# A projection moved ahead between two attention half-steps, and three PSUM banks taken in turn, in a fused attention and feed-forward block

## What is computed

```python
q = proj(query, Wq, bq)
k = proj(key, Wk, bk)
v = proj(value, Wv, bv)
scores = jnp.einsum('bhqd,bhkd->bhqk', q, k) / jnp.sqrt(jnp.asarray(dk, q.dtype))
p = jax.nn.softmax(scores, axis=-1)
x = jnp.einsum('bhqk,bhkd->bhqd', p, v)
x = x.transpose(0, 2, 1, 3).reshape(B, S, D)
return jnp.einsum('bsd,ed->bse', x, Wo) + bo
...
x = x + jnp.tanh(g_xattn[0]) * _L0_xattn_ref(_layernorm(x, axis=-1), ctx_1024, ctx_1024, ...)
x = x + jnp.tanh(g_ffn[0]) * _L0_ffn_ref(_layernorm(x, axis=-1), ...)
```

## Time and profile before

| | us |
|---|---|
| median of 3 runs | 1734.7 (1734.4 to 1735.49) |
| the profiled execution, its time | 1731.45 |
| its span, first to last instruction | 1729.3 |
| PE busy | 1601.9 (93%) |
| DVE busy | 1302.7 (75%) |
| ACT busy | 840.5 (49%) |
| POOL busy | 558.9 (32%) |

### The profile page before, as it was taken

How to read it: one execution, slowest core, us unless ns; L and a number is a source line. 1 busy time by engine, 2 the same in 40 slices (tenths; PEclk the granted TensorE clock), 3 DMA queues, 4 the chain that set the end, 5 groups by cost and what they waited for, 6 DMA issues and landing times.

```text
span 1729.3 us, 31276 instructions
## 1 busy us (share of the span) xinstructions
PE 1601.9 (93%) x11748; PEld 752.0 (43%) x11748; DVE 1302.7 (75%) x2085; ACT 840.5 (49%) x1122; POOL 558.9 (32%) x782
## 2 busy tenths in 40 slices
PE   4879999999999999999999999985999999989888
PEld 2334544444445444444454444433444444434333
DVE  5638788787887887878878778676687778778766
ACT  4443534535336344353353533524677777757440
POOL 5423514335234242351432523212000000008778
PEclk9989999999999999999999999999899999999999
DMA  8668769788687687886968777635344552027996
GB/s 243 167 173 180 176 160 206 166 199 171 179 182 185 171 191 179 193 176 170 204 160 203 174 180 141 168 71 198 116 183 182 207 200 98 25 82 296 424 413 229
DMA packets 301108, 320.75 MB, mean 185 GB/s; under 512 B 176432, under 2 KB 225584, under 8 KB 298032
## 3 DMA queue, kind: packets, MB, share of 16 engines
q1 hardware_dynamic: 299248, 318.72, 67.8%
q10 hardware_dynamic: 1728, 0.27, 0.1%
HBM read 180.49 MB, written 100.27 MB: 162 GB/s over the span
## 4 chain that ended last, share of the span: by engine, by line
PE 44%; issue 25%; DVE 11%; DMA 7%; ACT 6%; POOL 4%; SPq 3%; POOLq 0%; ACTq 0%; DVEq 0%
PE bank L1492 10%; PE bank L1380 10%; PE bank L1382 9%; PE bank L1381 9%; PE spair L1469 5%; DMA x<-out_dram 4%; DVE mx L1032 4%; POOL yh L712 3%; ACT pr L755 2%; PE spair L1444 2%; DMA stacks<-mT 2%; SPq L412 1%; ACT wf L825 1%; DVE wi L1120 1%; DVE bst L982 1%
## 5 line engine op out<-in xcount | busy, mean ns | idle before, releaser
L1032 DVE TENSOR_REDUCE mx<-spair 128x4 f32<-128x1024 f32 x256 | 301.1, 1217 | 33.9 <-PE spair L1444 33.4
L755 ACT ACTIVATE pr<-spair 128x1024 f32<-128x1024 f32 x256 | 258.0, 1019 | 125.4 <-PE spair L1469 125.4
L1009 DVE SCALAR_TENSOR_TENSOR parts<-bank,bqk,parts 128x512 f16<-128x512 f32 x128 | 96.0, 750 | 177.8 <-ACT parts L744 176.4
L1600 PE MATMUL spair<-xqT,wgT 128*128 128x512 bf16 x704 | 182.5, 382 | 1.0 <-ACT xqT L910 1.0
L1600 PE MATMUL spair<-xqT,wuT 128*128 128x512 bf16 x704 | 182.1, 381 | 0.0
L1469 PE MATMUL spair<-stacks 128*128 128x256 f16 x1024 | 154.2, 277 | 24.8 <-DMA stacks<-mT 14.4
L744 ACT ACTIVATE parts<-bank,bqk 128x512 f16<-128x512 f32 x128 | 87.7, 685 | 153.4 <-PE bank L1382 153.4
L868 ACT ACTIVATE sil<-spair,gsc 128x512 f32<-128x512 f32 x176 | 118.3, 680 | 78.8 <-PE spair L1600 78.7
L618 POOL TENSOR_TENSOR cl<-cbuf,ch 128x512 f16<-128x512 f32 x64 | 79.0, 1235 | 236.4 <-ACT ch L732 236.4
L712 POOL TENSOR_TENSOR yh<-yh,x 128x512 f32<-128x512 f32 x64 | 134.7, 2136 | 48.7 <-DVE yh L1328 25.0
L1492 PE MATMUL bank<-pr,v 128*32 128x256 f32 x2048 | 137.9, 387 | 12.3 <-ACT pr L755 7.6
(11 more groups left out here) (187 smaller groups left out, 3324.4 us busy)
## 6 DMA issues: line engine op xcount, KB each, us to landing
stacks<-qk_spill SPq DMA_DIRECT2D x384, 128.0 KB, 4.0
qk_spill<-parts SPq DMA_DIRECT2D x64, 512.0 KB, 5.1
x<-out_dram SPq DMA_DIRECT2D x32, 1024.0 KB, 11.1
h_spill<-hb SPq DMA_DIRECT2D x10, 2816.0 KB, 9.2
xbuf<-in_x_dram SPq DMA_DIRECT2D x16, 1024.0 KB, 7.2
cbuf<-in_ctx_dram SPq DMA_DIRECT2D x16, 1024.0 KB, 6.7
xres<-in_x_dram SPq DMA_DIRECT2D x16, 1024.0 KB, 5.6
out_dram<-xres SPq DMA_DIRECT2D x16, 1024.0 KB, 4.6
```

Of the source, the lines that this page charges most:

```text
L755: act.activation(pr[:, u % 4, :, :, :].rearrange("p a b q -> p (a b q)"), spair[u % 2][:, :, :].rearrange("p a q -> p (a q)"), ACT.Exp, sc ...
L1009: dve.scalar_tensor_tensor(out=parts[:, c, 2 * w + 1, :], in0=pj[(g + 1) % 3][:, :], scalar=bqk[:, w, c:c + 1], in1=parts[:, c, 2 * w, :], ...
L1032: dve.tensor_reduce(mx[:, h:h + 2, b, :], spair[u % 2][:, :, :].rearrange("p a (q k) -> p a q k", q=KH), AX_X, ALU.max).then_inc(max_done, 1)
L1600: last = pe.matmul(spair[k % 2][:, s, :], w[:, t, kc * P:kc * P + P], xqT[:, par, kc, :], start=(kc == 0), stop=(kc == KC - 1))
```

## The change

Four things change, all in attention bodies with a new group i.

1. On PE `qk(i, 2)` stands between `score(j, 1)` and `score(j, 2)`. In the loop over g each step takes the projection that the next step had: `qk(i, g + 3)` for g = 0 to 4, `vproj(i, 0)` for g = 5 and `vproj(i, 1)` for g = 6, where no projection stood within the loop.
2. After the loop there is one projection less. `max_pair(i, 0)` follows directly; `vproj` 2 and 3 have pairs 1 and 2 behind them, the four `oproj` pairs 3 to 6, and pair 7 follows pair 6.
3. The three banks are taken strictly in turn by the 16 projections of a body, through `turn_bank`. Since 16 is not a multiple of 3, the first bank moves by one from body to body.
4. The waits of `vproj` 0 to 2 name the `qk_low` that empties their bank in the new turn.

```diff
+        def turn_bank(i, k):
+            if i == 0:
+                return pj[(k + 1) % 3 if k < 8 else k % 3]
+            return pj[(i + k) % 3]
+
         def x1_bank(j, t):
-            return pj[t % 2] if j == LAST else pj[t % 3]
+            return pj[t % 2] if j == LAST else turn_bank(j + 1, 12 + t)
...
             def vproj(i, t, par):
                 if t < 3:
-                    wait(pe, qk_lo, i * 8 + (8, 6, 7)[t])
+                    wait(pe, qk_lo, i * 8 + ((8, 6, 7) if i == 0 else (6, 7, 8))[t])
                 else:
                     wait(pe, v_ready, i * NT + 1)
-                three(pj[(2 + t) % 3][:, :],
+                three(turn_bank(i, 8 + t)[:, :],
...
                 score(j, 0)
                 score(j, 1)
+                if i is not None:
+                    qk(i, 2, par, before)
                 for g in range(NGR - 1):
                     score(j, 2 * g + 2)
                     pv(j, g)
                     score(j, 2 * g + 3)
-                    if i is not None and g + 2 < 8:
-                        qk(i, g + 2, par, before)
+                    if i is not None:
+                        if g + 3 < 8:
+                            qk(i, g + 3, par, before)
+                        else:
+                            vproj(i, g - 5, par)
                     if i is None and g >= NGR - 3:
                         oproj(j, g - (NGR - 3), None)
                 if i is not None:
-                    vproj(i, 0, par)
                     max_pair(i, 0)
                 pv(j, NGR - 1)
                 if i is not None:
-                    for t in range(1, NT):
+                    for t in range(2, NT):
                         vproj(i, t, par)
-                        max_pair(i, t)
+                        max_pair(i, t - 1)
                 for t in range(NT) if i is not None else range(2, NT):
                     oproj(j, t, i)
                     if i is not None:
-                        max_pair(i, NT + t)
+                        max_pair(i, NT - 1 + t)
+                if i is not None:
+                    max_pair(i, 7)
```

More of the change, by code:

```diff
@@ L743, in qk_high @@
                 wait(act, spilled[c], i * 16)
-                act.activation(parts[:, c, 2 * w, :], pj[(g + 1) % 3][:, :], ACT.Identity,
+                act.activation(parts[:, c, 2 * w, :], turn_bank(i, g)[:, :], ACT.Identity,
                                bias=bqk[:, w, c:c + 1]).then_inc(qk_hi, 1)
@@ L748, in v_copy @@
                 wait(act, v_mm, i * NT + t + 1)
-                act.activation(v[:, t, :], pj[(2 + t) % 3][:, :], ACT.Copy, scale=1.0 / WS).then_inc(v_ready, 1)
+                act.activation(v[:, t, :], turn_bank(i, 8 + t)[:, :], ACT.Copy, scale=1.0 / WS).then_inc(v_ready, 1)
             def exps(j, u):
@@ L1008, in qk_low @@
                 wait(dve, qk_hi, i * 8 + g + 1)
-                dve.scalar_tensor_tensor(out=parts[:, c, 2 * w + 1, :], in0=pj[(g + 1) % 3][:, :], scalar=bqk[:, w, c:c + 1],
+                dve.scalar_tensor_tensor(out=parts[:, c, 2 * w + 1, :], in0=turn_bank(i, g)[:, :], scalar=bqk[:, w, c:c + 1],
                                          in1=parts[:, c, 2 * w, :], op0=ALU.add, op1=ALU.subtract).then_inc(qk_lo, 1)
@@ L1400, in qk @@
                     wait(pe, v_ready, i * NT)
-                three(pj[(g + 1) % 3][:, :],
+                three(turn_bank(i, g)[:, :],
                       [([wT[w][:, k, s, c * P:c * P + P] for s in range(2)], [src[:, k, s, :] for s in range(2)])
```

## The result

The changed kernel takes 1760.84 us in the median of 4 runs (1760.04 to 1761.88), against 1735.1 before (1734.4 to 1736.56): a ratio of 1.0148, with a 95% interval from 1.0136 to 1.016. It is slower by 25.7 us. The profiled execution took 1760.04 us and has a span of 1757.9, 28.6 longer than that of before.

The account below looks back on a forecast made before the run. PE was taken as 93% busy, in step with DVE in the tail from pair 4. Terms summed to +16.8 us without the clock, +30.3 with it: span 1759.6, carried to a median of 1765.0 us, range 1749 to 1777.

Parts of the forecast that it names:

- head, bodies 2 to 15: First score to first product: grows from 2.64 to 4.01 us, 14 x 1.37 = 19.2 us.
- middle: Fourth product's wait for DVE's third `norm`: 0.42 us goes in 13 bodies, -5.5 us, bounds -5.5 and 0.
- before pair 2: Start of the tail, PE's wait for DVE: 0.2 us of lead left per body, 15 x -0.2 = -3.0 us.
- last `oproj`: Bank turn in the tail: it waits for the first `x1_tile`, 0.24 us later, 15 x 0.24 = +3.6 us.
- pair 6 to 7: End of the tail: PE idles 2.5 us awaiting DVE's reductions, tail as long as before, 0 (-0.1 to +0.3 a body).
- clock: New idle stretch before pair 7: nine falls to half clock in 15 bodies, 1.5 us each, +13.5 us, bounds 0 and 22.5.
- The core: Tail and head: work that left the tail is replaced by 2.5 us standing; work put in the head is added.
- Rival A: Same steps, but the clock holds at the new idle stretch: +16.8, 1751.5 us; chance 0.20.
- Rival B: Filling head and middle stalls is pure gain, 23.5 us, 1711 us; needs under 1.2 us before pair 7; chance 0.03.
- Rival C: Even exchange: DVE's chain begins early enough to end all tail standing, +4.7, 1739.4 us; chance 0.04 together with E.
- Rival D: Nearly every stretch costs the clock and the transfer of the maxima is hindered more: +40, 1775 us; chance 0.11.
- Rival E: The bank turn could hold a projection at its old time: 1735 us; chance 0.04 together with C.

Follow-up runs that it names:

- The run with six matmuls: Kernel before, with the first six of the third projection's twelve matmuls between second and third half-step, six at the old place: 1720.41 us, ratio 0.9917.
- the one with half a place up to step 3: Six matmuls at the head as well as steps 0 to 2 taking half their own projection and half the next, step 3 one half: 1712.04 us, ratio 0.9868.
- the run with the short reduction: Kernel after, with the second reduction of pair 6 cut to 8 of 128 keys in groups 1 to 15: 1734.06 us, ratio 0.9994.
- the run with ten additional matmuls: Kernel after, with ten matmuls of unused result between pair 6 and pair 7, keeping PE busy: 1747.83 us, ratio 1.0067.
- the runs with nine and with twelve matmuls at the head: Kernel before, with nine or all twelve of the third projection's matmuls between second and third half-step: 1721.26 us and 1731.87 us.

## Why the prediction was right

Forecast 1765.0 us, measured 1760.84; forecast for the profiled span 1759.6, measured 1757.9. By its steps, each from starts of rows in the 15 bodies:

| step | forecast, us | in the profile after, us |
|---|---|---|
| head, bodies 2 to 15 | +19.2 | 14 x (4.00 - 2.64) = +19.0 |
| head, body 1, to the second product | +2.5 | +2.5 |
| middle | -5.5 | 13 x (5.43 - 5.86) = -5.6 |
| before pair 2 | -3.0 | 14 x -0.18 = -2.5, body 15 none |
| last `oproj` | +3.6 | 15 x (3.25 - 3.02) = +3.4 |
| pair 6 to 7 | 0 | 15 x (2.85 - 3.03) = -2.7 |
| clock | +13.5 | 8 x 1.58 = +12.6, the ninth at the end of body 15 +0.2 |
| first scores after `turn_max` | not in the sum | +1.8 in body 1, +0.4 in the others |

The right column adds up to 29.1 us; the spans differ by 28.6. Its last row is, as far as the runs tell, not the change's doing: over the profiles of all eleven kernels the first scores of body 1 come anywhere from 13.7 to 16.5 us after `turn_max`, and before had one of the two earliest. Without that row the steps give 26.9 us, beside 25.7 between the medians and 30.3 in the forecast.

*The core held.* The work taken out of the tail was replaced by standing, and the work put into the head was added, less what stood there. The run with the projection at the head alone shows it from the other side: there the empty place gives back 1.66 us a body and the kernel is not slower (1731.87), while the empty place in front of pair 7 gives back 0.18.

*The middle and the start of the tail held*, with their mechanisms: DVE's `qk_low` came earlier because the projections of steps 0 to 2 ended earlier. The run with six matmuls, in which only the third projection moves, kept the wait, and the one with half a place up to step 3 lost it. For the start of the tail there is no such run, only rows: in body 5 DVE's `piece_int` starts 0.27 us after pair 0 in before and 0.10 in after, each time behind ACT's rounding.

*Pair 6 to pair 7 was mis-sized*: 0 was forecast, with bounds of -0.1 to +0.3 us a body, and it is -0.18. I put pair 7 at 2.5 us of idle behind pair 6, which is what was measured (2.45), and so 0.11 us earlier than before, but then held `turn_max` to DVE's chain. It isn't held there: after pair 7 it is 2.93 us to `turn_max` with no idle time before it, just PE's own pair and projection, and so the 0.18 us came back in each body. Together with the 0.23 us of the bank, the tail from pair 5 to `turn_max` is 9.03 us where it was 8.98.

*The clock held in number and price.* Nine falls were forecast and nine came, which with 15 equal stretches is partly luck; the price, 1.5 us, was 1.58. Rival A, the same steps without the clock, gave 1751.5; the run in which PE is kept busy realises it, at 1747.83. Of the 3.7 us between, 2.7 are pair 7's. The rest comes from carrying a profiled span over to medians, less the late first scores (about 2 us): the profiled execution of before lay 3.3 us under its median, that of after only 0.8. This is also why the median is 4.2 us under the forecast when the span is only 1.7 under.

*Rival B* (filling idle time of the engine that is 93% busy is pure gain) named its point of decision, 1.2 us from pair 6 to pair 7; it was 2.45. *Rival C* needed DVE's chain to start early enough; the wait before pair 2 shrank by 0.18 us, not by 0.43 to 2. *Rival D* would have needed a fall in nearly every body. *Rival E*: the banks alone change nothing, and in bodies 2 to 15 of the kernel after the only projection that waits for its bank is the last `oproj`, 0.17 us. The Trainium skill's advice on idle gaps (TensorE: Matmul & The Clock Gate, HAM oscillation) draws the line too high for this kernel: gaps of 2.45 us, shorter than the ones it warns of, brought falls in nine of 15 bodies.

What my expectations had wrong was in the runs. The run with six matmuls was to bring the middle's 5.5 us too: I had not asked which projection the waiting instruction hangs on. The floor of step 0 was put down to the exponentials: I had not asked which other waits the next product has.

## What to carry to other kernels

When work moves into a stall from another place, price both ends: what it covers where it goes (only up to the length of the stall), and what had been leaning on it where it was. A producer and a consumer that alternate, as the pairs and their reductions do here, need something between two turns; the cheapest repair was not to move a whole unit but to cut it to the length of the stall, and to leave the gap where the engine next to it has slack. An idle stretch also has a price of its own on TensorE; here even matmuls without use inside it paid back 13 us.

## What the runs showed of the hardware

Fifteen idle stretches of 2.45 us each, in the same surroundings and after dense work, brought the granted clock to half (1.2 GHz) in nine cases and left it up in six; what sets the nine apart from the six stays open. Stretches of 1.42 us left it up in bodies 1 to 14 (the run with the short reduction), and stretches of 0.2 us in all 15 (the run with ten additional matmuls). In eight of the nine cases the fall cost 1.4 to 1.7 us before `turn_max`. In the runs with nine and with twelve matmuls at the head a product's bank was used again 3.77 us after the start of the product before, of which 1.87 us are PE's work and most of the rest DVE's four steps of `norm`.
